# A convolution with an expert network behind it: the turned gates go to DRAM a chunk ahead, and their broadcast is made in four parts

## What is computed

```
x = x + conv3x3(quant(ln_c(x)), quant(w))          # 4-bit fake quantisation of both
t = tokens(x)                                      # 8192 tokens of 64 channels
n = ln_t(t)
probs = softmax(n @ gate_w + gate_b)               # 8 experts
cw = probs where among the two largest, else 0
out = t + sum over e of cw[:, e] * (gelu(n @ W1[e] + b1[e]) @ W2[e] + b2[e])
```

## Time and profile before

| | us |
|---|---|
| median of 3 runs (lowest, highest) | 208.22 (204.78, 213.34) |
| the profiled execution | 207.22 |
| its span, first to last instruction | 205.4 |

### The profile page before, as it was taken

One profiled execution on the slowest core, in us unless ns is written; L12 is line 12 of the kernel. 1 busy time (PEld: TensorE's weight loads), 2 busy tenths in 40 slices (PEclk: granted clock), 3 DMA queues, 4 the chain that ended last, 5 costly groups with the idle time before them and its releaser, 6 DMA issues.

```text
span 205.4 us, 4030 instructions
## 1 busy us (share of the span) xinstructions
PE 170.1 (83%) x1214; PEld 86.0 (42%) x1214; DVE 146.9 (71%) x459; ACT 116.6 (57%) x153; POOL 125.1 (61%) x117
## 2 busy tenths in 40 slices
PE   2968489676849369899799999999979999999980
PEld 2956334443428324454344344444424443444320
DVE  0899999999978899669378368577458485354351
ACT  2447822235038829248977766666747766766630
POOL 7698135557726044244776757867727867578492
PEclk9997859999996958999999999999999999999996
DMA  6970000000000006948707929928919949749701
GB/s 178 314 102 0 3 2 0 2 2 0 3 0 0 0 10 149 205 97 191 177 20 190 219 58 226 215 91 183 206 56 212 216 121 191 159 126 202 186 3 51
DMA packets 16322, 22.41 MB, mean 109 GB/s; under 512 B 2345, under 2 KB 8113, under 8 KB 16305
## 3 DMA queue, kind: packets, MB, share of 16 engines
q1 hardware_dynamic: 16144, 22.04, 47.2%
q10 hardware_dynamic: 160, 0.15, 0.3%
HBM read 19.82 MB, written 2.36 MB: 108 GB/s over the span
## 4 chain that ended last, share of the span: by engine, by line
PE 35%; DVE 27%; DMA 18%; issue 9%; ACT 5%; SPq 2%; DVEq 1%; POOLq 1%; ACTq 0%
PE ps L1080 17%; PE ps L1097 16%; DMA gbc<-gate_rows 12%; DMA gate_rows<-gateT 4%; DVE ssum L615 4%; DVE xn L702 3%; DVE xn L721 3%; DVE xn L627 3%; DMA cw<-in_conv_w 2%; SPq L278 2%; DVE w_lo L675 2%; DVE gbc L698 1%; PE ps L1036 1%; ACT hl L490 1%; DVE topi L815 1%
## 5 line engine op out<-in xcount | busy, mean ns | idle before, releaser
L400 POOL TENSOR_TENSOR x<-x,y_sb 128x512 f32 (+1 forms) x63 | 80.2, 1273 | 41.6 <-DVE y_sb L854 37.1
L543 ACT ACTIVATE work<-ps,bias_sb,w_back 128x1024 f32<-128x1024 f32 x64 | 76.9, 1203 | 38.9 <-PE ps L1080 38.7
L854 DVE SCALAR_TENSOR_TENSOR y_sb<-ps,bias_sb,gbc 128x512 f32<-128x512 f32 x64 | 47.3, 746 | 42.6 <-PE ps L1097 27.7
L1097 PE MATMUL ps<-work,w_sb 128*64 128x512 f32 x256 | 65.8, 594 | 2.0 <-DVE y_sb L854 1.9
L1080 PE MATMUL ps<-xT,w_hi 128*64 128x512 f16 x256 | 39.7, 389 | 1.1 <-ACT work L543 1.1
L1080 PE MATMUL ps<-xT,w_lo 128*64 128x512 f16 x256 | 39.2, 385 | 0.0
L1080 PEld LDWEIGHTS ps<-xT,w_hi 128*64 128x64 f16 x256 | 13.8, 111 | 33.2 <-issue 30.6
L993 PE MATMUL ps<-qpad,cw_bd 128*128 128x512 bf16 x72 | 19.6, 425 | 7.7 <-POOL qpad L355 7.7
L1097 PEld LDWEIGHTS ps<-work,w_sb 128*64 128x64 f32 x256 | 17.8, 137 | 15.5 <-ACT work L543 5.1
L1080 PEld LDWEIGHTS ps<-xT,w_lo 128*64 128x64 f16 x256 | 15.1, 112 | 13.4 <-issue 1.0
L355 POOL TENSOR_TENSOR qpad<-work,xn 128x512 bf16<-128x512 f32 (+1 forms) x8 | 10.5, 1310 | 15.9 <-DVE work L727 15.9
(11 more groups left out here) (112 smaller groups left out, 186.9 us busy)
## 6 DMA issues: line engine op xcount, KB each, us to landing
gbc<-gate_rows SPq DMA_DIRECT2D x16, 768.0 KB, 9.9
gbc<-gate_rows SPq DMA_DIRECT2D x16, 256.0 KB, 4.0
x_sb<-in_x SPq DMA_DIRECT2D x8, 256.0 KB, 5.2
out<-x SPq DMA_DIRECT2D x8, 256.0 KB, 10.0
w_raw<-in_W SPq DMA_DIRECT2D x2, 256.0 KB, 6.2
w_sb<-in_W SPq DMA_DIRECT2D x1, 256.0 KB
gate_rows<-gateT SPq DMA_DIRECT2D x8, 32.0 KB, 4.2
cw<-in_conv_w ACTq DMA_DIRECT2D x2, 72.0 KB, 3.7
```

The costliest lines, as they stand in the source:

```text
L400: pool.tensor_tensor(x2[:, ds(c * W, W)], x2[:, ds(c * W, W)], y_sb[:, u % H_RING, :], ALU.add).then_inc(added, 1)
L543: act.activation(h_sb[:, u % H_RING, :], bank(H + 2 * (u % 2), 2 * W), ACT.Gelu, bias=b1_sb[:, u:u + 1], scale=w_back[:, u:u + 1]).then_in ...
L854: dve.scalar_tensor_tensor(y_sb[:, u % H_RING, :], bank(Y + u % 2), b2_sb[:, u:u + 1], gbc[:, slot, u, :], ALU.add, ALU.mult).then_inc(wei ...
L1097: last = pe.matmul(ps[r * CH:(r + 1) * CH, (Y + u % 2) * W:(Y + u % 2 + 1) * W], w2_sb[:, u, :], h_sb[:, u % H_RING, r * W:(r + 1) * W], s ...
```

## The change

The broadcast is in four parts of two experts. Each part waits until the same two units of the chunk that used the slot are weighed; the wait for the whole chunk is gone. TensorE turns the gates of chunk 2 behind unit 0 of chunk 1 (before: unit 1), and those of chunks 3 to 7 behind unit 7 of the chunk two before (chunk c+2 behind unit 7 of chunk c). ScalarE takes the gates of chunk c+1 behind the gelu of unit 0 of chunk c in place of unit 2. The loops over chunks on SyncE and ScalarE are written out. VectorE's list is as it was.

```diff
-GATE_PARTS = ((0, 2), (2, 8))
+GATE_PARTS = ((0, 2), (2, 4), (4, 6), (6, 8))
...
-        gbc_in = [[sem(f"gbc_in{s}{h}") for h in range(2)] for s in range(2)]
+        gbc_in = [[sem(f"gbc_in{s}{h}") for h in range(len(GATE_PARTS))] for s in range(2)]
...
                 if isinstance(c, int) and c < 2:
                     wait_alone(sp, (rows_out, 16 * (c + 1)))
                 else:
-                    wait_alone(sp, (rows_out, 16 * (c + 1)), (weighted, UNITS * (c - 1)))
+                    wait_alone(sp, (rows_out, 16 * (c + 1)))
                 for h, (first, last) in enumerate(GATE_PARTS):
+                    if c >= 2:
+                        wait_alone(sp, (weighted, UNITS * (c - 2) + last))
                     for r in range(2):
...
-            with sp.Fori(0, (NCH - 2) // 2) as i:
-                for s in range(2):
-                    spread_gates(2 * i + s + 2, s)
-                    store(2 * i + s)
+            for c in range(2, NCH):
+                spread_gates(c, c % 2)
+                store(c - 2)
...
-            def gelus(c, gates_after=2):
+            def gelus(c, gates_after=None, taken=0):
...
                     if u == gates_after:
-                        take_gateT(c + 1)
+                        take_gateT(taken)
...
-            gelus(0, gates_after=3)
+            gelus(0, gates_after=3, taken=1)
             exponentials(2)
...
-            with act.Fori(1, NCH - 1) as c:
-                gelus(c)
-            gelus(NCH - 1, gates_after=None)
+            gelus(1, gates_after=0, taken=2)
+            for c in range(2, NCH - 1):
+                gelus(c, gates_after=0, taken=c + 1)
+            gelus(NCH - 1)
...
-            def ffn(c, gates=True, first=False):
+            def ffn(c, first=False):
...
-                    if u == 1 and gates and not first:
-                        transpose_gates(c + 1)
+                    if c == 1 and u == 0:
+                        transpose_gates(2)
+                    if u == UNITS - 1 and 1 <= c <= NCH - 3:
+                        transpose_gates(c + 2)
```

More of the change, by code:

```diff
@@ L1136, in _ @@
                 ffn(c)
-            ffn(NCH - 1, gates=False)
+            ffn(NCH - 1)
             for u in range(UNITS - G2_LAG, UNITS):
```

## The result

The changed kernel takes 209.37 us, median of 20 runs (208.85 to 210.01), the kernel before 208.62 us, median of 20 runs (204.78 to 213.5). The ratio is 1.017, 95% interval 1.014 to 1.019: slower, by less than 2%. The forecast was 209.6 us. The ratio compares only the runs within 1.5% of the fastest of their kernel, which of the kernel before, as it scatters over 9 us where the changed one stays within 1.2 us, are 7 of 20; by the medians of all runs the change costs 0.4%.

A forecast was written before the change was run, and what follows sets the result against it. TensorE was taken to bound the kernel at 14.12 us a chunk. Span 205.4 - 3.2 + 5.1 = 207.3 us, plus 1.8 us outside it 209.1, half-way to the median 209.6 us; range 205.5 to 213.5 us.

The forecast's parts named there:

- The floor of 14.12 us for a chunk: From one transposition of gates to the next, TensorE's work sets at least 14.12 us per chunk of eight units.
- What the change gives back, 3.2 us of span: Late broadcasts gone: 2.2 us between transpositions, 0.4 in the last chunk, 0.6 at GpSimd's closing adds.
- the lead of 3.7 us: ScalarE takes chunk 3's gates near 112.8 us, not 116.48, so their broadcast lands in time.
- Rival E: Broadcasts stay late, as eight small transfers land no sooner than four; stalls stay: 212.3 us, chance 0.05.
- What the change costs, 5 x 1.02 = 5.1 us: In chunks 1 to 5 the moved transposition waits for VectorE's gates and TensorE stands 1.02 us each.
- The hold: GpSimd's add of unit 4 holds a VectorE routing operation; free of it, gates would be ready 1.03 us earlier.
- ScalarE's take: Taking the turned gates, 0.26 us, moves from behind unit 2 to behind unit 0 on an idling engine: nothing.
- the loops are worth nothing: Written-out loops on SyncE and ScalarE only take away register moves on engines that wait.
- B, no stall: Routing runs free of GpSimd's adds, so the moved transposition never waits: 204.0 us, chance 0.14.
- C, two holds: Routing held at two places by GpSimd's adds; each stall 1.8 us in the middle: 213.0 us, chance 0.15.
- D: Standing lets TensorE's clock fall, costing 8.6 us over five stalls: 218 us, chance 0.05.
- The half-way step of 0.5 us: Half of the 1.0 us between the profiled execution and the median of runs, taking 209.1 to 209.6 us.

The follow-up runs named there:

- e1: Changed kernel with the transposition of chunk c+1's gates behind unit 0 of chunk c, one unit later: 203.95 us, ratio 0.981 to the kernel before.
- e3: Changed kernel with transpositions and ScalarE's take put back as before; four parts, waits per part and written-out loops remain: 203.85 us, ratio 0.982.
- e7: Changed kernel with transposition behind unit 0 of chunk c, broadcast in two parts and whole-chunk wait as before; ScalarE's earlier take kept: 205.39 us, ratio 0.995.
- e4: Changed kernel with VectorE making the gates behind the weighing of unit 3 in place of unit 4: 204.24 us, ratio 0.983.
- e6: Changed kernel with transpositions one unit earlier still, behind unit 6: 217.45 and 220.68 us in two runs, rough ratio 1.068.
- e5: Changed kernel with GpSimd's add of unit 4 replaced by a fill that reads nothing, so unit 4's share is missing: 204.59 us.
- e9: e3 with four parts, but one wait for the whole chunk in place of the wait for each part: 204.11 us, ratio 0.989.
- e8: e3 with the broadcast in two parts and the whole-chunk wait; only the written-out loops remain of the change: 204.67 us, ratio 0.993.
- e2: Kernel before with only the transpositions moved as in the change; parts, waits and loops as before: 210.99 us, ratio 1.015.

## Why the prediction was right

**What bounds the kernel.** The floor of 14.12 us for a chunk, set by TensorE: right. The transpositions of e1 and e3 are 14.12 or 14.13 us apart without a single exception in the loop.

**What the change gives back, 3.2 us of span.** It measured 205.4 - 202.0 = 3.4 us (e3, the gain without the cost). All six waits for the broadcast went, as taken. But the reason given, the lead of 3.7 us, was not what did it: e7 has the lead and keeps waits, e3 has no lead and none. That the term came out right is luck: its size is TensorE's floor, which holds whatever brings the gates in time. The working took the landing times of the old, large transfers and started them earlier; it did not ask what the earlier write of the rows queues behind, nor what it means that unit 2 no longer waits for experts 4 to 7. Its landing times were far off too: for the gates of chunk 3 it had the first part there by 128.4 us and the last by 132.0 us, and they were there at 121.1 and 128.0 us in the changed kernel, with the rows landing in 1.8 us and not 4.2. Rival E named this place, but had it the wrong way round: eight smaller transfers do land sooner.

**What the change costs, 5 x 1.02 = 5.1 us.** The stretches grew to 15.12 us, 1.00 us each; from e3's span to the changed kernel's it is 207.0 - 202.0 = 5.0 us. The step-by-step arithmetic (product, weighing, routing, hand-over) put the first transposition at 111.55 us, it came at 111.52. e1 and e4 take the stall away from either side, e6 lengthens it by just the one unit.

**The hold.** The forecast said that 1.03 us of the chain were a hold by GpSimd's add. In e5 the chain from the start of the weighing (109.32 us) to the gates (110.84 us) is 1.52 us, in the changed kernel 2.54 us (108.92 to 111.46): 1.02 us less.

**The rest.** ScalarE's take and the waits for each part at no cost: right, as e1, e3 and e9 differ in them and their medians lie within 0.3 us. SyncE's eight issues at no cost: right, as e3 has them and no wait. That the loops are worth nothing was wrong for the old broadcast (e8), right for the new. The transposition in chunk 1 at no cost: as before, ScalarE loads a table twice there (1.28 us each, at 95.70 and 97.43 us), and TensorE waits for ScalarE until 100.07 us, for 0.99 us where it was 1.10.

**The rivals.** B, no stall: fell, but e4 and e5 are what it would have been, 204.2 and 204.6 us where it had 204.0. C, two holds: not in the changed kernel; it came once in e2, behind a late broadcast, with 1.82 us where its middle was 1.8. D fell by the clock in the changed kernel and in e6. E fell.

**The sum.** Its own figure was 209.1 us, on the scale of the first profiled execution, and half of the way to the median made 209.6; measured 209.37, the median of 20 runs. The span is the mechanism's own: 207.0 us in the profiled execution (209.96 us of device time), 207.2 us in the median of the runs, against the 207.3 forecast. The half-way step of 0.5 us had no cause behind it, and that it fits is luck. It stood for the scatter of the kernel before, which goes with the late broadcasts and is gone with them; on the scale of medians the late broadcasts cost more than 3.4 us (e3 is 4.6 us below the kernel before in the runs beside it). And the changed kernel has 2.1 us outside its span in the median run, where 1.8 was put in.

## What to carry to other kernels

When an instruction is moved forward on an in-order engine, count the work that remains between what its input waits for and its new place, and set it against the whole chain that makes the input, holds included: here 2.7 us of TensorE's work, from the start of unit 4's product (107.85 us) to the new place (110.59 us), stood against a chain of 3.7 us from the same start to the transposition (111.52 us), five times. A transfer that comes late is not cured by starting it earlier if the queue is full until then; first compare the time that one round of transfers takes with the length of a round, and look which piece the first waiting instruction really needs. And when a change has several parts, run each alone: here the part with the gain was two lines, and the part with the cost could be left out.

## What was not expected

The form of the broadcast seems to change what the DMA engines move at equal busy share: 226 to 236 GB/s in transfers of two experts (64 partitions x 2 x 512), 201 to 220 GB/s in transfers of six. These are single chunks of single profiles of e9 and e8, the chunk two later shows less of it, and why it is so stays open; it wasn't tried whether it is the size, the number of transfers in flight or the mixing with the store.

A write of 32 KB took 1.8 us to land with the queue empty (e9) and 7.1 us and more behind a broadcast (e7), on the same queue.

The medians of the kernel before in its five sets of runs, not all made on the same chip, were 208.62, 208.44, 206.41, 207.8 and 206.78 us, those of the kernels with four parts and no stall 203.85 to 204.6. With a kernel whose waits lie at the brink the choice of runs decides about as much as the change does.
